# In-degrees from positions in sorted targets, and five output banks in the first dense layer

## The reference

```python
weights = einsum('bsd,do->bso', x, wr) + br          # one score per node
idx = top_k(weights, k)[:k-1]                        # the chosen nodes
h = gelu(sel @ w1 + b1)                              # 256 -> 1024
y = (h @ w2 + b2) * w_sel                            # 1024 -> 256
out = zeros.at[idx].set(y) + x
```

```python
deg = segment_sum(ones_like(dst), dst, num_segments=n)   # dst holds the self loops too
norm = rsqrt(deg)[src] * rsqrt(deg)[dst]
out = segment_sum(h[src] * norm[:, None], dst) + b
```

## Time and profile before

| what | us |
|---|---|
| runs, median of three | 2884.21 (2881.09 to 2884.98) |
| the profiled execution | 2885.92 |
| its span, first to last instruction | 2884.0 |
| PE busy in the span | 2133.0 (74%) |
| DVE busy | 1697.5 (59%) |
| POOL busy | 1334.8 (46%) |
| ACT busy | 496.8 (17%) |

### The profile page before, as it was taken

One profiled execution on the slowest core, in us unless ns is written; L12 is line 12 of the kernel. 1 busy time (PEld: TensorE's weight loads), 2 busy tenths in 40 slices (PEclk: granted clock), 3 DMA queues, 4 the chain that ended last, 5 costly groups with the idle time before them and its releaser, 6 DMA issues.

```text
span 2884.0 us, 32702 instructions
## 1 busy us (share of the span) xinstructions
PE 2133.0 (74%) x9352; PEld 1536.8 (53%) x9353; DVE 1697.5 (59%) x4269; ACT 496.8 (17%) x1015; POOL 1334.8 (46%) x1321
## 2 busy tenths in 40 slices
PE   3467895667767767744598979989788888883897
PEld 3445674443443333633375756666566666661676
DVE  5865625455756653464466666553677777776343
ACT  3411221000101110030112121222211111110321
POOL 6000001777777730027776667500377777772000
PEclk8679997679989987876698989889778888886899
DMA  6000003334434323045554444400233333330100
GB/s 185 8 1 1 4 5 91 105 104 121 112 108 122 108 61 106 8 158 157 152 154 124 136 123 137 113 23 1 85 105 105 105 106 106 105 106 5 42 18 17
DMA packets 116745, 247.58 MB, mean 86 GB/s; under 512 B 34811, under 2 KB 60813, under 8 KB 116622
## 3 DMA queue, kind: packets, MB, share of 16 engines
q0 software_dynamic: 69216, 201.41, 25.4%
q1 hardware_dynamic: 44190, 44.69, 5.0%
q10 hardware_dynamic: 3216, 0.01, 0.1%
HBM read 224.34 MB, written 21.43 MB: 85 GB/s over the span
## 4 chain that ended last, share of the span: by engine, by line
PE 40%; POOL 27%; DVE 16%; issue 12%; ACT 3%; DMA 2%; DVEq 1%; SPq 0%; ACTq 0%; POOLq 0%; PEldq 0%
POOL BIG L419 26%; PE PB L772 6%; PE PB L761 6%; PE PB L572 3%; PE PB L538 3%; PE PB L635 3%; DVE ACC L1536 3%; PE PB L526 2%; PE PB L458 2%; PE PB L672 2%; PE PB L563 2%; PE PB L442 2%; DVE OH L1157 1%; PE PB L732 1%; PE PB L632 1%
## 5 line engine op out<-in xcount | busy, mean ns | idle before, releaser
L419 POOL DMA_INDIRECT BIG<-table,SRCI x832 | 830.9, 999 | 557.5 <-issue 243.1
L419 POOL DMA_INDIRECT BIG<-parts,SRCI x416 | 427.1, 1027 | 416.6 <-DMA parts<-BIG 236.4
L1536 DVE TENSOR_TENSOR ACC<-ACC,PB 128x256 f32 x832 | 349.8, 420 | 452.9 <-PE PB L635 189.2
L632 PE MATMUL PB<-BIG,OH 128*128 128x256 f32 x832 | 261.2, 463 | 110.1 <-DMA BIG<-table,SRCI 78.1
L872 PE MATMUL PB<-BIG,WA 128*128 128x264 f32 x832 | 271.7, 473 | 80.3 <-DVE ACC L1966 50.4
L635 PE MATMUL PB<-BIG,OH 128*128 128x256 bf16 x1248 | 196.8, 309 | 130.1 <-DMA BIG<-parts,SRCI 97.8
L632 PEld LDWEIGHTS PB<-BIG,OH 128*128 128x128 f32 x832 | 179.3, 230 | 187.1 <-DMA BIG<-table,SRCI 88.2
L872 PEld LDWEIGHTS PB<-BIG,WA 128*128 128x128 f32 x832 | 179.9, 233 | 134.2 <-DVE ACC L1966 83.4
L635 PEld LDWEIGHTS PB<-BIG,OH 128*128 128x128 bf16 x1248 | 132.7, 109 | 194.8 <-DMA BIG<-parts,SRCI 96.6
L1966 DVE TENSOR_TENSOR ACC<-ACC,PB 128x264 f32 x416 | 176.5, 424 | 37.1 <-PE PB L872 18.1
L772 PE MATMUL PB<-WB,HT 128*128 128x256 f32 x800 | 192.9, 384 | 6.9 <-DVE X L1796 6.4
(11 more groups left out here) (428 smaller groups left out, 3071.8 us busy)
## 6 DMA issues: line engine op xcount, KB each, us to landing
BIG<-table,SRCI POOLq DMA_INDIRECT x832, 2.8
BIG<-parts,SRCI POOLq DMA_INDIRECT x416, 3.1
table<-ACC SPq DMA_DIRECT2D x10, 660.0 KB, 3.4
swtab<-HT SPq DMA_DIRECT2D x25, 256.0 KB, 2.5
BIG<-swtab SPq DMA_DIRECT2D x5, 1280.0 KB, 11.9
parts<-BIG SPq DMA_DIRECT2D x5, 960.0 KB, 4.1
X<-in_x SPq DMA_DIRECT2D x1, 3072.0 KB
out<-X SPq DMA_DIRECT2D x4, 640.0 KB
```

The lines of the kernel that those rows point to most:

```text
L419: g.indirect_dma_start(out=ring[:, k * width:(k + 1) * width], out_offset=None, in_=rows, in_offset=bass.IndirectOffsetOnAxis(ap=SRCI[:, n ...
L632: mm = pe.matmul(to, OH[:, h * P:(h + 1) * P], G[:, r * ROW:r * ROW + D], start=True, stop=True)
L1536: v.tensor_tensor(dst, dst, bank[:, k % 2 * D:(k % 2 + 1) * D], ALU.add).then_inc(sem(f"{st}_acc"), 1)
```

## The change

Two things are changed. The degrees no longer come from one-hots. `dst` is sorted, so the number of edges with a target up to node v is a position. The first number of each of the 128 rows of `dst` is spread over the partitions by one product; DVE compares these heads with every node (one operation over 25 x 128 elements), which gives the last row whose head is not above the node. POOL then gathers this row of 392 numbers for each node (25 gathers of 128 rows, into ACC, a ring of 16), and DVE counts the numbers up to the node (`within`, one compare with an accumulator per tile). Row number times 392 plus that count is the position. Eight of the 25 compares run in the search, the other 17 in chunk 1. Three small products give the position of the node before, and the difference is the degree. The totals by tile and their running sum fall away: they are the positions of each tile's last node.

And in f0 the outputs of a chunk use five banks, the waits for DVE are moved to hidden blocks 0 and 1 of the next chunk, the turns of the next chunk stand between the outputs, and chunk 1 is normalised before the search.

```diff
-        def f0_bank(c, j):
-            return PB[((1, 6) if c + 1 < NC else (7, 6))[j % 2]]
+        def f0_bank(j):
+            return PB[(2, 3, 4, 1, 5)[j]]
...
+        drows = lambda t: ACC[:, t % D_RING * SPAN:(t % D_RING + 1) * SPAN].bitcast(I32)
...
@@ POOL, behind the gathers of x @@
+            g.wait_ge(sem("d_given"), 2)
+            for t in range(NT):
+                if t >= D_RING and t % 4 == 0:
+                    g.wait_ge(sem("d_within"), t - D_RING + 4)
+                g.indirect_dma_start(out=drows(t), out_offset=None, in_=a["dst"].rearrange("(p c) -> p c", p=P),
+                                     in_offset=bass.IndirectOffsetOnAxis(ap=DIDX[:, t:t + 1], axis=0)).then_inc(sem(f"d_in{t // 4 % 4}"), 16)
...
@@ PE @@
-            for n in range(H_EARLY):
-                count(n)
+            pe.wait_ge(sem("d_given"), 1)
+            pe.matmul(PB[7][:, 0:P], HEADS, IDENT[:, :], start=True, stop=True).then_inc(sem("d_spread"), 1)
...
@@ hidden @@
+                    if c and h < 2:
+                        pe.wait_ge(sem(f"{st}_out"), (c - 1) * CH + (2, CH)[h])
...
@@ output @@
-                    n = c * CH + j
-                    if n > 1:
-                        pe.wait_ge(sem(f"{st}_out"), n - (0 if j == 0 else 1))
...
@@ after hidden block h of chunk c @@
-                        for n in range(done, done + H_AT_HIDDEN[c]):
-                            count(n)
+                        if c == D_LAST + 1 and h == 0:
+                            pe.wait_ge(sem("d_given"), 3)
+                            pe.matmul(PB[7][:, 0:NT], PREV, BYNODE[:, 1:NT + 1], start=True, stop=False)
+                            pe.matmul(PB[7][:, 0:NT], WRAP, BYNODE[:, 0:NT], start=False, stop=True)
+                            pe.matmul(PB[7][:, 64:64 + NT], LAST, BYNODE[:, 1:NT + 1], start=True, stop=True).then_inc(sem("d_spread"), 1)
...
-                    if c + 1 < NC:
-                        for j in range(CH):
+                    for j in range(CH):
+                        if c + 1 < NC:
                             turn(st, c + 1, j, 0, 1)
-                    pe.wait_ge(sem(f"{st}_act"), c * 8 + 8)
-                    if c == 0:
-                        pe.wait_ge(sem("sel_done"), 1)
-                    elif c == NC - 1:
-                        pe.wait_ge(sem("slots_ready"), 1)
-                    for j in range(CH):
+                        if j == 0:
+                            pe.wait_ge(sem(f"{st}_act"), c * 8 + 8)
                         output(c, j)
...
@@ before project("g1") @@
+            pe.wait_ge(sem("f0_out"), NT)
+            pe.wait_ge(sem("slots_ready"), 1)
...
@@ DVE, at the start @@
+            v.tensor_copy(HEADS, dst2[:, 0:1].to_broadcast([P, P])).then_inc(sem("d_given"), 1)
+            v.wait_ge(sem("d_spread"), 1)
+            line.step(v, v.tensor_tensor(BELOW.rearrange("p (t n) -> p t n", t=NT), PB[7][:, 0:P].unsqueeze(1).to_broadcast([P, NT, P]),
+                                         NODE[:, :].unsqueeze(2).to_broadcast([P, NT, P]), ALU.is_le))
+            line.step(v, v.tensor_reduce(BYNODE[:, 1:NT + 1], BELOW.rearrange("p (t n) -> p t n", t=NT), AX.X, ALU.add))
+            line.step(v, v.tensor_scalar(BYNODE[:, 1:NT + 1], BYNODE[:, 1:NT + 1], -1.0, 0.0, ALU.add, ALU.max))
+            v.tensor_copy(DIDX[:, :], BYNODE[:, 1:NT + 1]).then_inc(sem("d_given"), 1)
+            def within(t):
+                if t % 4 == 0:
+                    v.wait_ge(sem(f"d_in{t // 4 % 4}"), 16 * (t // D_RING * 4 + min(4, NT - t)))
+                if t:
+                    v.wait_ge(sem("d_within"), t)
+                v.tensor_scalar(WITHIN, drows(t), NODE[:, t:t + 1], 0.0, ALU.is_le, ALU.add,
+                                accum_out=BYNODE[:, NT + 1 + t:NT + 2 + t]).then_inc(sem("d_within"), 1)
...
@@ DVE, before the search @@
-            for j in range(CH):
-                ln_apply("f0", 0, j, True)
+            for c in range(2):
+                for j in range(CH):
+                    ln_apply("f0", c, j, True)
...
@@ DVE, search step k @@
-                for n in range(done, done + H_AT_HIDDEN[0]):
-                    count(n)
+                for t in range(k * D_AT_STEP, (k + 1) * D_AT_STEP):
+                    within(t)
...
@@ DVE, chunk c, before its outputs @@
-                if c + 1 < NC:
+                if 0 < c < NC - 1:
                     for j in range(CH):
                         ln_apply("f0", c + 1, j, True)
+                if c == D_LAST:
+                    for t in range(8 * D_AT_STEP, NT):
+                        within(t)
+                    v.scalar_tensor_tensor(BYNODE[:, 1:NT + 1], BYNODE[:, 1:NT + 1], float(SPAN), BYNODE[:, NT + 1:2 * NT + 1],
+                                           ALU.mult, ALU.add).then_inc(sem("d_given"), 1)
...
@@ DVE, after the outputs of chunk D_LAST, in place of the copy of the counts after chunk 2 @@
+                    v.wait_ge(sem("d_spread"), 2)
+                    line.step(v, v.tensor_tensor(DEG[:, :], BYNODE[:, 1:NT + 1], PB[7][:, 0:NT], ALU.subtract))
+                    line.step(v, v.tensor_scalar(DEG[:, :], DEG[:, :], 1.0, None, ALU.add))
```

More of the change, by code:

```diff
@@ L43 @@
 AHEAD = 5
[L44 to L48, removed]
+D_RING = 16
+D_AT_STEP = 1
+D_LAST = 1
+SPAN = ET * P // P
 def tiles_before(st):
@@ L395, in _ @@
                             pattern=[[-P, NT]], channel_multiplier=-1).then_inc(sem("cst"), 1)
+            g.iota(NODE[:, :], pattern=[[P, NT]], base=0, channel_multiplier=1, allow_small_or_imprecise_dtypes=True).then_inc(sem("cst"), 1)
+            for to, base, step in ((PREV, 1, -1), (WRAP, 1 - P, -1), (LAST, 1 - P, 0)):
+                g.affine_select(out=to, in_=ONES[:, :], compare_op=ALU.is_equal, fill=0.0, base=base,
+                                pattern=[[step, P]], channel_multiplier=1).then_inc(sem("cst"), 1)
             g.wait_ge(sem("ld_idn"), 32)
@@ L576, in chosen_ffn @@
                 for j in range(CH):
-                    turn(st, 0, j, 0, 1)
+                    turn(st, 0, j, 0, 2)
                 pe.wait_ge(sem("ld_f0"), 16 * 6)
-                done = H_EARLY
                 for c in range(NC):
@@ L1016, in _ @@
             for j in range(CH):
-                to_xt(st, 0, j, 0, 1)
+                to_xt(st, 0, j, 0, 2)
             for c in range(NC):
@@ L1164, in _ @@
-            for n in range(H_EARLY):
-                count(n)
+            v.tensor_copy(HEADS, dst2[:, 0:1].to_broadcast([P, P])).then_inc(sem("d_given"), 1)
+            v.wait_ge(sem("cst"), 10)
+            v.wait_ge(sem("d_spread"), 1)
+            line.step(v, v.tensor_tensor(BELOW.rearrange("p (t n) -> p t n", t=NT), PB[7][:, 0:P].unsqueeze(1).to_broadcast([P, NT, P]),
+                                         NODE[:, :].unsqueeze(2).to_broadcast([P, NT, P]), ALU.is_le))
+            line.step(v, v.tensor_reduce(BYNODE[:, 1:NT + 1], BELOW.rearrange("p (t n) -> p t n", t=NT), AX.X, ALU.add))
@@ L1388, in _ @@
             line.step(v, v.tensor_tensor(SURE, SURE, SELGE[:, 0:NT], ALU.add))
-            v.tensor_tensor(COEF[:, :], COEF[:, :], SURE, ALU.mult).then_inc(sem("sel_done"), 1)
-            v.wait_ge(sem("sel_done"), 1)
+            line.step(v, v.tensor_tensor(COEF[:, :], COEF[:, :], SURE, ALU.mult))
             for c in range(NC):
-                if c:
-                    for n in range(done, done + 8 * H_AT_HIDDEN[c]):
-                        count(n)
-                    done += 8 * H_AT_HIDDEN[c]
-                if c + 1 < NC:
+                if 0 < c < NC - 1:
                     for j in range(CH):
                         ln_apply("f0", c + 1, j, True)
-                else:
+                if c == D_LAST:
+                    for t in range(8 * D_AT_STEP, NT):
+                        within(t)
+                    v.wait_ge(sem("d_within"), NT)
+                    line.sync(v)
+                    v.scalar_tensor_tensor(BYNODE[:, 1:NT + 1], BYNODE[:, 1:NT + 1], float(SPAN), BYNODE[:, NT + 1:2 * NT + 1],
+                                           ALU.mult, ALU.add).then_inc(sem("d_given"), 1)
+                if c == NC - 1:
                     own_scale("g1", c - 1)
```

82 lines of the change are left out of this document (14 added, 68 removed).

## The result

| | before | changed |
|---|---|---|
| median of 4 runs each | 2883.36 us (2881.09 to 2884.98) | 2799.19 us (2797.84 to 2801.41) |
| ratio | | 0.9704, 95% interval 0.9692 to 0.9715 |
| profiled execution, its span | 2885.9, 2884.0 | 2797.84, 2796.1 |
| mean granted clock | 0.843 | 0.850 |
| f0, from its first hidden block to its last output | 278.3 us | 199.4 us |

A forecast was written before the change was run, and what follows sets the result against it. PE's chain in f0 was taken as the bound. Gains in the search, the way to the first output and chunks 0 to 3 summed to 81.4 us: 2885.9 became 2804.5, and the median, 1.7 lower, 2803; range 2795 to 2816.

The forecast's parts named there:

- seven search intervals: Search in f0: steps fall from 3.20 to 2.7 us, so 23.2 becomes 19.7, a gain of 3.5 us.
- search to first output: Between search and first output, PE needs only the last sums and one turn: 2.5 us instead of 10.1, gain 7.6.
- chunks 1, 2, 3: f0's chunks of 64.4, 55.0 and 44.5 us were to fall by 27.2, 17.4 and 7.3 us.
- The first rule's example: Chunk 0's outputs before: clock 0.84 with PE pauses of 2.4 us per tile, read as short idles making the clock swing.
- The compare: DVE's compare over 392 int32 numbers with accumulator, in search and chunk 1: put at 0.65 us, bounds 0.36 and 0.74.
- The start of the search: Chunk 1's normalisation moves ahead of the search: at most 0.4 us lost, put at 0.
- The second rule: Two-port mode for DVE's compare: if it held with the accumulator, step 2.5 us and gain 1.4 us more.
- The start-up: At the kernel's start, a compare and a reduce over 3200 elements, 4.6 us each, 9.2, covered by DVE's idle time.
- the first (DVE as bound): Compare takes 1.5 us, so search steps take 3.6 and PE waits in chunk 1: 2813 us; chance 0.07.
- The third (a lower clock under dense work): Chip holds PE at 1.2 GHz through f0's dense 170 us: 2977 us; chance 0.02.
- the fourth (turns wholly hidden): Compare at its lower bound and turns between outputs wholly hidden: 2796 us; chance 0.05.
- The second: Turns between outputs wait for ACT, or the clock falls once per chunk: 2815 us; chance 0.15 with milder forms.

The follow-up runs named there:

- e1: New degrees with the order of before (two output banks, turns ahead of outputs), against the kernel before: 3196.61 us on another chip, ratio 0.9881.
- e2: Kernel before with five banks, turns between outputs and early normalisation of chunk 1, counts kept: 3208.48 us on another chip, ratio 0.9949.
- e11: e1 run again on a chip of the first kind, against the kernel before: 2821.27 us, ratio 0.978.
- e12: Changed kernel with the five turns of the next chunk ahead of the outputs, on a chip of the first kind: 2819.84 us, ratio 0.9781.
- e10: Changed kernel with all 25 compares in chunk 1 and none in the search: 2800.48 us, ratio 0.9704.
- e8: e7 with chunk 1's normalisation split, two tiles into the first search step and three behind COEF: 2796.18 us, ratio 0.9676.
- e7: Changed kernel, waiting for a chunk's last GELU only before the first output's eighth product, ACT's roots moved behind its copies and GELUs: 2797.21 us, ratio 0.9687.
- e9: Changed kernel with each of its 25 compares made twice, the second into a scrap tile: 2810.6 us, ratio 0.974.
- e3: Changed kernel with outputs in two banks instead of five and a wait for the tile before the last: 3179.01 us on another chip, ratio 0.9823.

## Why the prediction was right

The forecast was 2803 us in 2795 to 2816; 2799.2 was measured. The medians lie 84.2 us apart, where the sum gave 81.4. The mechanism was the forecast one; what was wrong in it is small and partly cancels, and is named below. Step by step, against the profiled executions:

| step | predicted | measured |
|---|---|---|
| seven search intervals | 19.7 | 20.2 |
| search to first output | 2.5 | 2.2 |
| outputs of chunk 0 | 18.4 | 18.15 |
| chunks 1, 2, 3 | 37.2, 37.6, 37.2 | 37.5, 38.1, 37.5 |
| first output at | 181 | 178.6 |
| last output ends | 351 | 349.3 |

- *The chunks.* The method was to take the last chunk of before, which had no counts and no turns between its parts, as the measure for all. It held to 0.5 us a chunk. e1, e2, e11 and e12 show why: the counts' pauses and the turns' pauses both cost their own length, the turns' pauses also cost clock behind them (e12), and with both gone the clock is 1.00.
- *The first rule's example* does not hold as it was read. The prediction put the clock of 0.84 in chunk 0's outputs down to the pauses of 2.4 us at each tile. In e2 the same pauses stand between the same tiles, and the clock is 1.00 there. e2 lacks the slow row of turns ahead of them (the stretch at 0.73); whether that makes the difference is not shown. The sum did not hang on it, since it took the whole part as measured.
- *The compare* was taken at 0.65 us and took 0.61; 0.54 is what it costs in the search. The bounds of 0.36 and 0.74 held it.
- *"PE needs 2.16 and at most 0.4 for the search's own product, so DVE still paces"* had PE's share right (2.56 against 2.54 measured) and the conclusion wrong. The compare cost 0.54 and not 0.65, so DVE needs no more time than PE, and PE paces, as e10 shows: a step is 2.54 and not 2.7. Over the steps this was worth 0.8 us, which the start of the search took back.
- *The start of the search, put at 0,* hid 1.5 us of loss, and that the interval sum still came near is in part luck. PE idled 2.04 us before the first product, its next block took 3.97 us instead of 2.40, and the first interval was 4.06 instead of 2.54. Against the predicted 7 x 2.7 + 0.8 that interval lost 1.4, the five of 2.54 won 0.8 back, and the long one (3.47, predicted 3.5) nothing, so 20.2 instead of 19.7. The granted clock of the two stretches, 149.88 to 156.21 and 156.21 to 160.22:

```profile
149.88:156.21 6.33, 4.29 (x9) 2.50 (x9) 5.90 (x27) 2.10 (x3) 0.00 (x0) 0.70 0.01 3
156.21:160.22 4.01, 4.01 (x11) 2.68 (x12) 2.84 (x11) 0.00 (x0) 0.00 (x0) 0.61 0.00 0
```

  The level was the lower one, 1.2 GHz, for most of that block. The prediction had priced one more slow block at 2.2 us and left it out of the sum; it came, for 1.5. In e8, which splits the normalisation of chunk 1, PE does not idle there, the same block takes 2.40 us, and f0 is 3.5 us shorter than in e7. The Trainium skill, "TensorE: Matmul & The Clock Gate", section "A second HAM failure mode: psum-queue depth-cycling", says that frequent short idles between groups of matmuls make the clock swing between its two levels. The block of 3.97 us behind the idle time and the one of 2.40 without it agree with that.
- *The perf mode.* The second rule, from "VectorE: DVE Perf Modes" in the Trainium skill, section "What auto-detection actually checks", lets a single-source operation between SBUF tiles take a two-port mode. The prediction asked whether it holds with an accumulator. The compare's 0.61 us against 0.36 for the plain operation of the same width shows no gain from it, but the two differ in more than the accumulator, and by e10 a shorter compare would have brought nothing.
- *The start-up* was covered. The compare and the reduce over 3200 elements took 3.5 us each, 7.0 against an upper value of 9.2, and DVE still waited for the gathered rows behind them. DVE's timeline of the changed kernel:

```profile
9.49 3.49 DVE L1135 TENSOR_TENSOR OH<-PB,NODE 128x3200 bf16<-128x3200 f32 x1 [1.03 <-PE PB L478]
...
13.02 3.48 DVE L1137 TENSOR_REDUCE BYNODE<-OH 128x25 f32<-128x3200 bf16 x1
...
25.60 3.36 DVE L1244 BATCH_NORM_STATS2 SMALL<-BIG 128x6 f32<-128x256 f32 x10 [5.08 <-DMA BIG<-in_x,IDN]
```

- *Not in the sum:* f0 began 2.65 us earlier (first turn 146.04 against 148.69), 1.0 of it from the start-up, where 26.60 became 25.60. With it the two medians are accounted for (81.2 and 2.65 against 84.2), and it is why the measured time lies under the forecast. The other 1.65 may be chance: the first turn lies between 146.0 and 148.2 in the nine profiles of kernels with the new degrees on this kind of chip. From the first turn to the end of the last output it is 81.2 us, against 81.4 predicted. (From the first hidden block it is 78.9, because that block now starts 2.4 us sooner after the first turn, and then waits for DVE.)

Of the rivals, the first (DVE as bound) fell by the compare's 0.54 us, where it needed 1.5; e9 shows that twice the load would have made it true in the search, and not in chunk 1. The third (a lower clock under dense work) fell by the clock of 1.00 over 174 us, and the fourth (turns wholly hidden) by the 0.22 us that each turn still takes (182.06 to 182.28). The second did not happen, but e12 shows that its mechanism is real, clock and all: it is what the changed order avoids. The prediction did not say which edit brings what; the runs do: in f0, 61 to 62 us for the degrees, 19 to 20 for the places of the turns, and 0 for the five banks.

## What to carry to other kernels

Look for a stretch in the same trace that already does the work without the disturbance, and price the disturbed ones by it: that gave every large term here to within 0.5 us, clock included. A row of short pauses on PE is to be priced with what the clock may take behind it; here four pauses of 0.56 to 1.18 us in a row made the next 17.5 us of products 1.6 to 2.4 us longer. It is no fixed price: single pauses, and the five longer ones of e2's chunk 0, took nothing. And before an order is spread over more buffers, ask how long the buffer is waited for: here not at all.

## What the runs showed of the hardware

- *Short pauses can lower the clock of a busy stretch behind them.* e12: outputs at 0.87 to 0.91 after four pauses, three or four of them of 0.56 us; e9: pauses of 0.4, 1.28 and 1.57 us, then a first output of 4.78 instead of 3.62 us. The changed kernel, with single pauses of 0.5 to 1.1 us, kept 1.00 from the end of the search on, and so did e2 in chunk 0's outputs, with a pause of 2.4 us behind each tile of 3.62 us. So the length of the pauses alone does not decide it; what does is open.
- *A compare with an accumulator over 392 int32 numbers* takes 0.61 us, and 0.08 for reading the accumulator, against 0.36 for a plain operation of the same width. How much of this is the accumulator's is not shown: the compare also takes its limit per partition and writes bf16, and an operation with per-partition operands and no accumulator takes 0.41 us over only 256 numbers.
- *One chip was slower by 350 us, and not in the rate of f0's work* (199.5 us in e3 there, 199.4 elsewhere). The kernel before took 3237.9 us there and 2883 to 2887 on the others. Most of it lies in the gather-bound stages: the stage named above took 884 to 896 us there against 782 to 786, and the one behind it 1493 to 1526 against 1317 to 1324. The rest lies ahead of f0. The profiles taken there hold many waits that no event of the trace explains, beside the gathers of the first stage; the changed kernel's own profile has one long one there, of 23.0 us on PEld. The waits of e3 there, from 30 to 212 us (engine, line and what it waited for: total, times, longest), and a row of its timeline:

```profile
PEld PB L487 <- issue: 76.4, 4, 30.2
ACT XT L983 <- remote: 60.5, 3, 32.0
...
DVE SMALL L1262 <- issue: 33.3, 1, 33.3
```
```profile
83.27 0.16 DVE L1262 COPY SMALL<-PB 128x4 f32<-128x4 f32 x1 [33.34 <-issue]
```

  The first turn of f0 comes at 205.3 to 206.6 us there in the three kernels with the new degrees and at 187.7 in e2 with the counts; on the other chips it comes at 146.0 to 148.7. So on that chip the new degrees gave back some 18 to 19 us ahead of f0, by one profile of each kernel, and e3, whose f0 is as long as the changed kernel's, was 59 us faster than the kernel before and not 84 (ratio 0.982; a gain of 84 would be 0.974 there). That the 25 gathers behind the 50 of x are the cause is only argued; the run that held them back was on another chip.
